# Softmax weighing moved to GpSimd for two batches, a new term order in the first product, and new queue orders

## Time and profile before

| | |
|---|---|
| time, median of 3 runs | 601.98 us (601.77 to 601.99) |
| the profiled execution: its own time / its span | 601.74 us / 599.9 us |
| TensorE busy | 591.1 us (99%) |
| VectorE / ScalarE / GpSimd busy | 488.4 / 328.0 / 44.1 us |
| granted TensorE clock (mean) | 1.0 |

### The profile page before, as it was taken

How to read it: one execution, slowest core, us unless ns; L and a number is a source line. 1 busy time by engine, 2 the same in 40 slices (tenths; PEclk the granted TensorE clock), 3 DMA queues, 4 the chain that set the end, 5 groups by cost and what they waited for, 6 DMA issues and landing times.

```text
span 599.9 us, 7168 instructions
## 1 busy us (share of the span) xinstructions
PE 591.1 (99%) x2635; PEld 273.0 (45%) x2635; DVE 488.4 (81%) x465; ACT 328.0 (55%) x478; POOL 44.1 (7%) x59
## 2 busy tenths in 40 slices
PE   8999999999999999999999999999999999999998
PEld 3444434544444444444444444444444444444446
DVE  4999999989989999989847958929795349999730
ACT  3999999954884553555358654344521041364421
POOL 0000021100000000110001011001100000011100
PEclk9999999999999999999999999999999999999999
DMA  8978887988887089868676858935842020376773
GB/s 324 362 207 209 250 175 153 324 216 245 160 242 165 5 185 280 211 174 217 135 164 135 218 107 200 217 74 123 92 78 42 0 47 7 71 123 105 133 127 58
DMA packets 148211, 95.43 MB, mean 159 GB/s; under 512 B 134352, under 2 KB 134736, under 8 KB 142800
## 3 DMA queue, kind: packets, MB, share of 16 engines
q1 hardware_dynamic: 142704, 66.92, 46.8%
q0 software_dynamic: 5472, 28.05, 20.5%
HBM read 26.81 MB, written 10.49 MB: 62 GB/s over the span
## 4 chain that ended last, share of the span: by engine, by line
PE 79%; DVE 0%; DVEq 0%; issue 0%
PE bank L785 49%; PE bank L797 17%; PE bank L800 9%; PE bank L765 2%; PE bank L815 1%; PE bank L820 1%; DVE dn L1592 0%; DVEq L108 0%; DVE W L1777 0%; DVEq L1775 0%
## 5 line engine op out<-in xcount | busy, mean ns | idle before, releaser
L785 PE MATMUL bank<-gu_hi,xT 128*128 128x512 f16 x1024 | 244.2, 379 | 1.2 <-DMA xT<-hT 1.2
L785 PEld LDWEIGHTS bank<-gu_hi,xT 128*128 128x128 f16 x1024 | 100.1, 98 | 122.2 <-DMA xT<-hT 1.9
L785 PE MATMUL bank<-gu_lo,xT 128*128 128x512 f16 x512 | 131.4, 379 | 0.0
L797 PE MATMUL bank<-dn,hT 128*128 128x512 f16 x480 | 106.0, 379 | 0.0
L1169 ACT ACTIVATE silu<-bank,unscale 128x512 f32<-128x512 f32 x64 | 43.5, 683 | 91.1 <-PE bank L785 37.1
L1731 DVE SCALAR_TENSOR_TENSOR h<-bank,unscale,silu 128x512 f32<-128x512 f32 x64 | 46.7, 746 | 41.4 <-PE bank L785 35.2
L785 PEld LDWEIGHTS bank<-gu_lo,xT 128*128 128x128 f16 x512 | 50.1, 98 | 60.4
L797 PEld LDWEIGHTS bank<-dn,hT 128*128 128x128 f16 x480 | 47.0, 98 | 56.6
L984 ACT ACTIVATE mag<-h 128x2048 bf16<-128x2048 f32 x18 | 34.3, 1903 | 50.4 <-DVE h L1748 27.6
L1541 DVE SCALAR_TENSOR_TENSOR h<-mag,h 128x2048 f32<-128x2048 bf16 x18 | 41.2, 2288 | 21.5 <-ACT mag L984 21.5
L800 PE MATMUL bank<-dn,hT 128*128 128x512 f16 x240 | 54.2, 379 | 0.0
(11 more groups left out here) (149 smaller groups left out, 580.2 us busy)
## 6 DMA issues: line engine op xcount, KB each, us to landing
W<-hT POOLq DMA_DIRECT2D x12, 1024.0 KB, 6.0
W<-in_units SPq DMA_DIRECT2D x11, 1024.0 KB, 6.7
h<-W POOLq DMA_DIRECT2D x7, 1024.0 KB, 6.4
h<-in_xcols SPq DMA_DIRECT2D x4, 1024.0 KB, 6.2
out_y<-y POOLq DMA_DIRECT2D x12, 256.0 KB, 4.4
h<-in_xrows SPq DMA_DIRECT2D x2, 1024.0 KB, 11.1
h<-hT POOLq DMA_DIRECT2D x2, 1024.0 KB, 8.0
out_y<-h SPq DMA_DIRECT2D x2, 1024.0 KB, 11.5
```

The costliest lines, as they stand in the source:

```text
L785: last = pe.matmul(bank[:, :], xT[:, b % 2, part, k, :], w[:, c, g, j * 512:(j + 1) * 512], start=(j == 0 and not low), stop=(j == HT - 1 ...
L797: pe.matmul(bank[:, :], hT[:, r % 2, 0, k, :], dn[:, w, k, :], start=(k == 0 and w == 0), stop=False)
```

## The change

GpSimd gets a `weigh` of its own for batches 2 and 3, with a semaphore of its own; ScalarE keeps it for 0 and 1. In the first product the high-half terms of gate and up come first, and then the two low x high terms. Besides, every written-out order is new: loads, transposes, GpSimd's queue, TensorE's, ScalarE's, VectorE's, the list of products and the banks.

```diff
+    pool_weighed = (2, 3)
+    act_weighed = (0, 1)
...
+        pool_normal_ready = sem("pool_normal_ready")
...
+            load_consts()
             load_slice(0)
-            load_consts()
             load_ctx(0)
             load_half(0)
             load_rest(0)
+            load_ctx(1)
+            load_unit(1)
             load_rows(0)
-            load_unit(1)
-            load_ctx(1)
+            load_ctx(3)
+            load_ctx(2)
+            load_unit(2)
+            load_rows(3)
+            load_columns(0)
             load_rows(1)
-            load_ctx(2)
-            load_rows(3)
-            load_unit(2)
-            load_columns(0)
+            load_columns(1)
             load_rows(2)
             sp.wait_ge(*unit_rest_in(0))
...
+            def weigh(b, nt):
+                pool.wait_ge(rsum_ready, b + 1)
+                row = slice(LT * b + nt, LT * b + nt + 1)
+                nc.gpsimd.tensor_scalar(probs[b][:, nt, :], probs[b][:, nt, :], rsum[:, row], None, ALU.mult
+                                        ).then_inc(pool_normal_ready, 1)
...
             unit_max(1)
+            unit_max(2)
             unit_rest(0)
-            unit_max(2)
             pool.wait_ge(wT_in[1], 16)
             unit_rest(1)
-            pool.wait_ge(wT_in[1], 32)
+            weigh(2, 0)
+            weigh(2, 1)
+            weigh(2, 2)
+            weigh(2, 3)
+            pool.wait_ge(wT_in[0], 48)
             unit_rest(2)
             rows_rest(0)
             unit_max(3)
-            unit_max(4)
+            weigh(3, 0)
+            weigh(3, 1)
             pool.wait_ge(wT_in[1], 48)
             unit_rest(3)
+            weigh(3, 2)
+            weigh(3, 3)
+            unit_max(4)
+            bound_max(3)
             pool.wait_ge(wT_in[1], 64)
             rows_rest(1)
-            bound_max(3)
             unit_max(5)
-            pool.wait_ge(nT_in[1], 32)
+            pool.wait_ge(nT_in[0], 32)
             unit_rest(4)
             unit_max(6)
-            unit_max(7)
...
-                pe.wait_ge(normal_ready, LT * b + nt + 1)
+                if b in pool_weighed:
+                    pe.wait_ge(pool_normal_ready, LT * pool_weighed.index(b) + nt + 1)
+                else:
+                    pe.wait_ge(normal_ready, LT * act_weighed.index(b) + nt + 1)
...
-                for g in range(2):
-                    bank = take_bank(f"{'gu'[g]}{r}.{c}")
-                    for part, w, low in ((0, gu_hi, None), (0, gu_lo, (wT_in[1], 32 * (c + 1))),
-                                         (1, gu_hi, (nT_in[1], 16 * (b + 1)))):
-                        if low and g == 0:
-                            pe.wait_ge(*low)
-                        for j in range(HT):
-                            k = (r % LT) * HT + j
-                            last = pe.matmul(bank[:, :], xT[:, b % 2, part, k, :], w[:, c, g, j * 512:(j + 1) * 512],
-                                             start=(j == 0 and not low), stop=(j == HT - 1 and part == 1))
-                    last.then_inc((gate_ready, up_ready)[g], 1)
+                terms = ((0, gu_hi, None), (0, gu_lo, (wT_in[1], 32 * (c + 1))), (1, gu_hi, (nT_in[1], 16 * (b + 1))))
+                passes = [((0, 1), terms[:2]), ((0, 1), terms[2:])] if (r, c) == products[0] else [((0,), terms), ((1,), terms)]
+                banks_of = {}
+                for gs, some in passes:
+                    for g in gs:
+                        if g not in banks_of:
+                            banks_of[g] = take_bank(f"{'gu'[g]}{r}.{c}")
+                        for part, w, low in some:
+                            if low and g == 0:
+                                pe.wait_ge(*low)
+                            for j in range(HT):
+                                k = (r % LT) * HT + j
+                                last = pe.matmul(banks_of[g][:, :], xT[:, b % 2, part, k, :],
+                                                 w[:, c, g, j * 512:(j + 1) * 512],
+                                                 start=(j == 0 and not low), stop=(j == HT - 1 and part == 1))
+                        if some[-1] is terms[2]:
+                            last.then_inc((gate_ready, up_ready)[g], 1)
...
             product(1, 0)
+            turn_probs(3, 0)
             product(0, 0)
             product(3, 0)
+            turn_probs(3, 1)
+            turn_probs(3, 2)
+            turn_probs(3, 3)
             product(2, 0)
             product(2, 1)
-            turn_probs(3, 0)
-            turn_probs(3, 1)
-            turn_probs(3, 2)
-            product(3, 1)
-            turn_probs(3, 3)
             product(0, 1)
+            product(1, 1)
             attend(3, 0)
             attend(3, 1)
             attend(3, 2)
             attend(3, 3)
+            product(6, 1)
+            product(5, 1)
...
             center_by_scalar(1, 1)
-            attended_variances(1, 0)
-            exponential(3, 3)
+            silu_of(1, 0)
             unit_hi(3)
             row_means(3, 1)
+            take_probs(3, 0)
+            silu_of(0, 0)
+            attended_variances(1, 0)
+            rows_magnitude(1)
             row_variances(3, 0)
+            unit_lo(3)
+            silu_of(3, 0)
+            take_probs(3, 1)
+            attended_variances(1, 1)
+            take_probs(3, 2)
             row_variances(3, 1)
-            rows_magnitude(1)
-            unit_lo(3)
-            attended_variances(1, 1)
-            silu_of(1, 0)
-            silu_of(0, 0)
-            weigh(3, 0)
+            take_probs(3, 3)
+            rows_hi(1)
             unit_magnitude(4)
-            silu_of(3, 0)
-            weigh(3, 1)
-            weigh(3, 2)
-            rows_hi(1)
-            weigh(3, 3)
+            unit_rescale(4)
+            x_scale(3)
             silu_of(2, 0)
-            take_probs(3, 0)
+            xt_hi(3)
             silu_of(2, 1)
-            unit_rescale(4)
-            take_probs(3, 1)
-            x_scale(3)
-            xt_hi(3)
-            take_probs(3, 2)
-            take_probs(3, 3)
             rows_lo(1)
-            silu_of(3, 1)
+            silu_of(0, 1)
...
-            row_max(0, 1)
             unit_reduce(1)
             unit_power(0)
+            row_max(0, 1)
             row_max(0, 2)
+            unit_round(0)
             row_max(0, 3)
-            unit_round(0)
+            row_max(1, 0)
+            row_max(1, 1)
...
+            row_max(3, 0)
             center(0)
+            unit_dequant(2)
             rows_scale(0)
-            unit_dequant(2)
-            add_attended(1, 0)
+            unit_reduce(3)
             rows_round(0)
             rows_dequant(0)
-            unit_reduce(3)
-            row_max(3, 0)
+            add_attended(1, 0)
             unit_largest(3)
+            row_max(3, 1)
...
```

More of the change, by code:

```diff
@@ L608, in _ @@
             turn_hidden_hi(14)
+            load_last()
             turn_hidden_lo(14)
@@ L872, in _ @@
             attend(1, 2)
+            attend(1, 3)
             turn_probs(2, 0)
-            energies(3, 0)
-            attend(1, 3)
             turn_probs(2, 1)
-            energies(3, 1)
             turn_probs(2, 2)
             turn_probs(2, 3)
+            energies(3, 1)
             energies(3, 2)
@@ L938, in _ @@
-            product(7, 3)
+            product(10, 2)
+            product(10, 3)
+            product(10, 0)
+            product(10, 1)
+            down(0)
+            down(1)
+            product(9, 2)
+            product(11, 2)
+            product(11, 1)
             product(11, 0)
             down(2)
-            product(8, 1)
-            product(11, 2)
+            down(3)
             product(11, 3)
-            down(3)
-            product(11, 1)
             down(4)
             product(12, 0)
-            product(13, 1)
+            product(12, 3)
@@ L949, in _ @@
+            product(12, 2)
+            product(12, 1)
+            down(5)
             product(14, 3)
[L950 to L952 removed]
             down(6)
[L954 removed]
             product(13, 3)
[L956 to L960 removed]
             product(13, 2)
             product(13, 0)
+            product(13, 1)
+            down(7)
+            product(14, 1)
@@ L963, in _ @@
+            product(15, 3)
+            product(14, 0)
+            product(15, 0)
+            down(8)
+            down(9)
+            product(14, 2)
+            product(15, 1)
             product(15, 2)
-            down(8)
-            product(15, 0)
-            down(9)
-            product(15, 1)
             down(10)
@@ L1379, in _ @@
             hidden_rescale(0)
+            hidden_magnitude(1)
+            silu_of(7, 1)
+            unit_rescale(10)
             silu_of(4, 2)
-            silu_of(4, 0)
-            hidden_magnitude(1)
+            unit_lo(9)
+            unit_magnitude(10)
+            hidden_hi(0)
+            silu_of(8, 1)
+            silu_of(8, 2)
+            silu_of(8, 0)
+            silu_of(8, 3)
```

(50 more changed lines are left out.)

708 lines of the change are left out of this document (337 added, 371 removed), and 10 rows, old and new, of the table products.

## The result

The change makes the kernel slower: 609.66 us (median of 4, 607.7 to 609.91) against 601.88 us for the kernel before on the same chip, a ratio of 1.0122, 95% interval 1.011 to 1.0135. The forecast was 604.6 us, range 600.5 to 607.5: the direction was right, and +7.8 us instead of +2.6 is outside the range. One execution behind this document was slow (the profiled one of run a1, 626.63 us at a granted clock of 0.95 throughout); a1's times are those of its other three.

The account below looks back on a forecast made before the run. TensorE, busy 591.1 of 599.9 us, was taken as the bound; early gains are lost because ScalarE's extra table loads start `attend(3, 0)` 2.6 us later, moving 601.74 to 604.3, plus 0.24 for the median: 604.6 us, range 600.5 to 607.5.

Parts of the forecast that it names:

- the first product: First feed-forward product on TensorE: starts at 85.4 us again and ends at 90.6 instead of 91.8.
- Loads: Loads at the start: context 1 lands at 10.6 us instead of about 15.6; TensorE some 1.5 us ahead there.
- GpSimd's DMA of rows 0: Accumulating DMA before the first product: goes out near 74.8 us, SyncE turns the high half near 80.6 as before.
- Term order: In the first product: 16 high-half matmuls ahead of the low half instead of 8, so the 1.2 us wait goes.
- ScalarE's step: Up to `xt_hi(3)`: eight table loads instead of 3, ending at 125.4 us, so `attend(3, 0)` starts 2.6 us later, at 127.9.
- GpSimd's weighings: Eight weighings moved from ScalarE: 0.8 us each on GpSimd, nothing on TensorE's path; batch 2's hidden up to 3.2 us each.
- Rival 1: ScalarE in time at `attend(3, 0)`, the counted loads falling away: 1.7 us faster, 600.3 us; chance 0.20.
- Rival 2: GpSimd and VectorE block each other during weighings, delaying the first product and `xt_hi(3)`: 607 us; chance 0.12.
- Rival 3: A stage behind 128 us (a bank, unit 7, a hidden row) is late: about 2 us more, 606.6; chance 0.09.
- Rival 4: Each table load also drains ScalarE, 1.4 us more for each of five loads: 611 us; chance 0.02.

Follow-up runs that it names:

- a1: Kernel after the change with unit 0's first slice loaded ahead of the constants again: 607.7 us, ratio to before 1.0083.
- b1: Kernel before with the constants loaded ahead of unit 0's first slice, nothing else: 604.19 us against 601.83, ratio 1.0034.
- c1: Kernel after with the first slice ahead of the constants and one hand-loaded table for Ln and Exp: 602.83 us, ratio to before 1.0018.
- a2: Kernel after with one table for Ln and Exp loaded ahead of the Ln of `attended_variances(1, 1)`: 604.61 us, ratio to before 1.0052.
- a3: Kernel after with 56 small unread matmuls on TensorE before the first product: 611.45 us, ratio to before 1.0157.
- a4: Kernel after with 28 small unread matmuls on TensorE before the first product: 607.87 us, ratio to before 1.0103.
- c2: Kernel after with first slice ahead of the constants, one hand-loaded table for Ln and Exp, and GpSimd's eight multiplications left out: 601.11 us, ratio to before 1.0002.
- d2: Kernel before with new term order, only batch 3 weighed on GpSimd, behind `unit_rest(3)`, `row_sum(3)` two steps earlier, `unit_max(4)` where it was: 607.07 us.
- b2: Kernel before with the new order of terms in the first product alone: 601.89 us, ratio 1.0001.
- b4: Kernel before, its orders kept, with the new term order and batches 2 and 3 weighed on GpSimd: 619.67 us, ratio 1.0303.
- a5: Kernel after with GpSimd's eight multiplications left out, batches 2 and 3 going on unweighed: 607.6 us, ratio to before 1.0113.
- b3: Kernel before with the new term order and the table for Ln and Exp loaded ahead of `x_scale(3)`: 600.96 us, ratio 0.9985.

## Why the prediction was wrong

**The step that failed** is the first product: "the product starts at 85.4 again", and "ends at 90.6". It started at 89.96 and ended at 97.0, 6.4 us late, and `attend(3, 0)` was then 5.6 us behind the forecast. Three terms of it failed and one held:

- *Loads.* I priced what moved ahead of context 1 and nothing for context 0. The constants (321 KB) and the slice (128 KB) stand ahead of it in either order, so the bytes in the queue are the same, and so I left it out. Yet the first projection starts at 7.73 us, where that of before started at 5.97 (line below), and `rows_dequant(0)` ended at 74.98 instead of the 72.8 of my walk: 2.2 us. a1 (-2.0) and b1 (+2.4) show that the swap does it, and in c1, with the slice first, `rows_dequant(0)` ends at 73.02. Part of it is the halved clock behind the first wait. Why context 0 lands later with the same bytes is open.

```profile
5.97 3.96 PE L739 MATMUL bank<-gu_hi,gu_lo 128*128 128x512 f32 x8
```

- *GpSimd's DMA of rows 0* went out 1.25 us behind the end of `rows_hi(0)` (76.93), where I had 0.1, and the high half was ready for SyncE 7.3 us after its issue instead of 5.8. The faster transpose issue behind it (1.81 us instead of 2.74) gave back 0.35. 2.2 + 1.15 + 1.5 - 0.35 = 4.5 of the 4.6 us. In the kernels with the orders of before this took 5.8 to 6.0 us every time, in those with the new ones 6.1 to 7.5. It also varies between executions of one order: in a2, a3 and a4 the same orders gave an issue 0.6 to 0.9 us behind `rows_hi(0)` and 6.4 to 6.7 us to the turn, so about 1 us of the lateness belongs to the execution that was profiled. The weighings aren't needed for it (c2: 7.5 us without them). All this is read from the traces, with no experiment that isolates it; its cause is open.
- *The clock.* 7.04 us for the product instead of 5.18: 1.86 us. The prediction had no term for it; no wait in the trace of before is over 1.21 us, and the clock is 1.0 throughout. c2 and d2 show the same behind waits of 3.24 and 4.16 us, and a4 prices it: the same start at full clock, and `attend(3, 0)` 1.67 us earlier.
- *Term order.* This held: no wait inside the first product. But b2 shows that alone it is worth nothing, because `attend(3, 0)` is then late.

**ScalarE's step, said to decide, was right.** Eight loads, as counted (both kernels load the table of both functions at the start, which is why Ln and Exp at 104.08 us load nothing in the earlier trace rows; the first silu replaces it); `xt_lo(3)` 2.35 us and `attend(3, 0)` on its end; the wait for `silu_of(2, 0)` in `product(1, 1)`. With a late start of 6.4 us instead of none, the whole walk from the first product ended 0.8 us earlier than I had it. The terms that the experiments on the kernel after give: table loads 5.1 us (a2; in the profiled executions 3.0 of them are clock and an earlier first product), swap of loads 2.0, GpSimd 1.7 (c1 less c2, by the ratios 1.0). c1 confirms the sum of the first two, not how the clock is to be split between them; the last term is a difference to c2, so that the three lead to c2's 601.11 us confirms nothing more. The kernel before has 601.7 there: the other new orders and the term order together win 0.6 us, inside the interval of c2, so no gain of theirs is shown, and that with 4.9 us less work on ScalarE.

**GpSimd's weighings**: I took 0.8 us each and bounded them at 3.2 by the cover. The four of batch 2 took 2.17 us each (after) to 3.3 us (b4), near the bound, and the switches of 5.7 to 7.8 us weren't in any bound. TensorE waits for it only in runs where the first product is earlier than in the profiled execution (a2, c1: 1.7 us), and in the orders of before (b4). The Trainium skill ("GPSIMD Engine Reference", 3.1 Elementwise) gives 769 ns for 512 elements as the best case, a tight loop; this case's trace has 2170 ns, and the measurement decides. The same page (2.1 Instruction dispatch) says that the first call to freshly loaded code costs about 6 us with no visible instruction; the 5.7 to 7.8 us before each change between reduction and multiplication in these runs are about that and more, and would fit if each change reloads, which the page doesn't say and no run tests.

**The rivals.** Rival 1 was ruled out by the eight loads. Rival 2, blocking: VectorE's instructions beside the weighings are longer only here and there (0.67 us instead of 0.20 in b4, 2.76 instead of 2.29 in the kernel after); it is GpSimd's that vary. Two stretches of b4 show by how much (columns as above):

```profile
57.40:70.70 13.30, 11.63 (x37) 5.50 (x35) 13.09 (x12) 10.45 (x18) 13.29 (x5) 1.00 0.88 237
108.30:111.45 3.15, 1.54 (x8) 0.49 (x5) 0.00 (x0) 0.00 (x0) 3.14 (x3) 1.00 0.00 0
```

Beside a busy VectorE four weighings take 13.32 us, 3.3 us each; with VectorE and ScalarE idle two take 3.13, 1.6 us each. So GpSimd is slowed by what runs beside it. Which of the two does it isn't separated, but VectorE isn't held for a weighing's length. The 607 us that the rival gave was closer, by another mechanism. Rival 3: nothing behind 133 us was late. Rival 4: 609.66 is near its 611, and it is still wrong. Ln (0.29 us) and the next load stand right behind a load at 123.96, with no drain between. A right total doesn't make a mechanism right; the row does.

## What to carry to other kernels

Price every change to the loads ahead of the first instruction of the bounding engine, even a swap of two small ones: in b1 nothing hid it, and it was carried to the end (1.2 us in the profiled execution, about 2 by the medians). A wait of TensorE in a kernel at full clock must be priced with what comes behind it: 1.86 us more behind the wait of 3.2 us here, so two delays that each look harmless could together cost more than their sum (argued, no run tries it). And work moved to an idle engine brings its queue with it: list what stands behind each moved instruction on the new engine and what it waits for (13.5 us in b4), and give a switch of GpSimd between kinds of operation a price of its own.

## What the runs showed of the hardware

- The granted clock fell to 0.5 with waits of TensorE of 2.08, 2.25, 2.32, 2.80, 3.20, 3.24, 4.16, 7.70 and 13.5 us, and stayed at 1.0 with waits of 1.21, 1.43, 1.67, 1.73, 1.83 and 1.99 us. One case (a5, a wait of 1.96 us at the start) is unclear: the view shows 1.00, yet twelve matmuls take 8.29 us, 0.69 each, where eight take 3.67, 0.46 each, in b1.
- A table that holds both Ln and Exp exists; where it isn't loaded by hand, the two functions alternate between two tables, 1.28 us each time (113.01 behind 111.40). The Trainium skill ("ScalarE: Activation LUTs", Table sets: the hidden batching unit) counts one load for Ln and then Exp; the trace agrees only where the table is loaded by hand (a2, b3).
- The same GpSimd multiplication (128x512, float32) takes 1.6 us with VectorE and ScalarE idle and 3.3 us with VectorE all but always busy (b4).
- An accumulating DMA of 1 MB from GpSimd's queue took 5.8 to 6.0 us from its issue to its reader with one set of queue orders and 6.1 to 7.5 us with the other; the cause is open.
